# A pair of indirect transfers that waits for one landing of the pair in front

## What is computed

```python
x = L0_attn_x
x = x + 0.5 * _L0_ffn_ref(_layernorm(x, axis=-1), ...)
x = x + _L0_attn_ref(_layernorm(x, axis=-1), ...)
x = x + 0.5 * _L0_ffn_ref(_layernorm(x, axis=-1), ...)

def _L0_ffn_ref(x, gate_w, gate_b, w1, b1, w2, b2):
    logits = jnp.einsum('bsd,ed->bse', x, gate_w) + gate_b
    probs = jax.nn.softmax(logits, axis=-1)
    topk_vals, topk_idx = jax.lax.top_k(probs, K)
    h = jax.nn.relu(jnp.einsum('bsd,edh->bseh', x, w1) + b1)
    expert_out = jnp.einsum('bseh,eho->bseo', h, w2) + b2
    sel = jnp.take_along_axis(expert_out, topk_idx[..., None], axis=2)
    return jnp.sum(sel * topk_vals[..., None], axis=2)
```

## Time and profile before

| | |
|---|---|
| median of 3 runs | 1311.96 us (1311.27 to 1317.21) |
| the profiled execution | 1328.29 us |
| its span on the core | 1326.6 us |
| mean granted TensorE clock in it | 0.941 |
| busy: PE, ACT, DVE, POOL | 1202.2, 960.0, 688.8, 470.4 us |
| indirect transfers (software queue q0) | 31.49 MB, 7.9% of 16 engines |
| plain transfers (hardware queue q1) | 168.90 MB, 41.3% of 16 engines |

### The profile page before, as it was taken

One profiled execution on the slowest core, in us unless ns is written; L12 is line 12 of the kernel. 1 busy time (PEld: TensorE's weight loads), 2 busy tenths in 40 slices (PEclk: granted clock), 3 DMA queues, 4 the chain that ended last, 5 costly groups with the idle time before them and its releaser, 6 DMA issues.

```text
span 1326.6 us, 25770 instructions
## 1 busy us (share of the span) xinstructions
PE 1202.2 (91%) x8269; PEld 793.0 (60%) x8269; DVE 688.8 (52%) x2239; ACT 960.0 (72%) x2383; POOL 470.4 (35%) x528
## 2 busy tenths in 40 slices
PE   7988889989899998999999979998999989999696
PEld 2675576576466555666656546655755446666475
DVE  4357437456576543546573446544647636455133
ACT  3337759669699886887988857887868888797431
POOL 2012324344344434413443444343343442243333
PEclk9987998989989998999999979999998979999888
DMA  7305473664644264555557455626641145656561
GB/s 257 142 13 164 144 219 94 195 191 130 191 131 141 82 208 128 151 162 180 165 159 213 126 153 175 191 86 205 180 131 36 43 135 163 187 166 198 187 213 55
DMA packets 159849, 202.04 MB, mean 152 GB/s; under 512 B 16922, under 2 KB 103394, under 8 KB 159715
## 3 DMA queue, kind: packets, MB, share of 16 engines
q1 hardware_dynamic: 144196, 168.90, 41.3%
q0 software_dynamic: 15360, 31.49, 7.9%
q10 hardware_dynamic: 160, 0.01, 0.0%
HBM read 152.49 MB, written 47.84 MB: 151 GB/s over the span
## 4 chain that ended last, share of the span: by engine, by line
DMA 36%; PE 23%; issue 15%; POOL 14%; ACT 7%; DVE 4%; SPq 0%; POOLq 0%; DVEq 0%; ACTq 0%
PE psum L1548 21%; DMA Y<-results_A,posA 11%; DMA slots_C<-xnC,posC 9%; DMA Y<-results_C,posC 8%; POOL Y L1096 8%; DMA slots_A<-xnA,posA 7%; POOL slots_C L1076 3%; POOL slots_A L1076 3%; ACT psum L1177 3%; ACT probs L1168 2%; DVE neg_m L1502 1%; DVE X L1467 1%; ACT xnA L1133 1%; PE psum L1657 1%; PE psum L1625 0%
## 5 line engine op out<-in xcount | busy, mean ns | idle before, releaser
L1502 DVE TENSOR_REDUCE neg_m<-psum 128x1 f32<-128x512 f32 x512 | 317.0, 681 | 199.4 <-PE psum L1548 165.6
L1548 PE MATMUL psum<-nat 32*128 32x512 f32 x2048 | 393.8, 671 | 18.3 <-ACT psum L1177 13.6
L1177 ACT ACTIVATE psum<-psum,neg_m 128x512 f32<-128x512 f32 x512 | 341.5, 683 | 42.4 <-DVE neg_m L1502 35.7
L1168 ACT ACTIVATE probs<-psum 128x512 f32<-128x512 f32 x512 | 266.7, 632 | 35.1 <-PE psum L1548 33.2
L1548 PEld LDWEIGHTS psum<-nat 32*128 32x128 f32 x2048 | 144.7, 193 | 116.6 <-ACT psum L1177 36.1
L1076 POOL DMA_INDIRECT slots_A<-xnA,posA x120 | 117.5, 979 | 261.8 <-DMA slots_A<-xnA,posA 117.9
L1548 PEld LDWEIGHTS psum<-xg_T,wt 128*128 128x128 f32 x1296 | 161.3, 198 | 55.4 <-issue 15.7
L1548 PE MATMUL psum<-xg_T,wt 128*128 128x128 f32 x1296 | 179.1, 287 | 16.4 <-DMA wt<-packed 11.0
L1096 POOL DMA_INDIRECT Y<-results_C,posC x120 | 114.5, 954 | 207.5 <-DMA Y<-results_C,posC 138.5
L1096 POOL DMA_INDIRECT Y<-results_A,posA x120 | 114.7, 956 | 200.3 <-DMA Y<-results_A,posA 156.0
L1548 PEld LDWEIGHTS psum<-wt,hg 128*128 128x128 f32 x1296 | 158.8, 199 | 40.1 <-issue 14.3
(11 more groups left out here) (188 smaller groups left out, 1339.8 us busy)
## 6 DMA issues: line engine op xcount, KB each, us to landing
wt<-packed SPq DMA_DIRECT2D x324, 320.0 KB
xs<-slots_A SPq DMA_DIRECT2D x36, 256.0 KB
results_A<-ys SPq DMA_DIRECT2D x36, 256.0 KB
xs<-slots_C SPq DMA_DIRECT2D x36, 256.0 KB
results_C<-ys SPq DMA_DIRECT2D x36, 256.0 KB
X<-in_L_attn_x_dram SPq DMA_DIRECT2D x16, 256.0 KB, 7.0
out_dram<-X SPq DMA_DIRECT2D x16, 256.0 KB
packed<-probs SPq DMA_DIRECT2D x1, 2560.0 KB, 7.8
```

The source lines that it names most:

```text
L1168: act.activation(probs[:, kt, j, :], at.banks()[j][:], ACT.Exp).then_inc(a_done, 1)
L1177: act.activation(at.banks()[j][:], at.banks()[j][:], ACT.Exp, bias=neg_m[:, g, n, j:j + 1], accum_out=sums[:, g, n, j:j + 1]).then_inc(S[" ...
L1502: V_.tensor_reduce(neg_m[:, g, n, j:j + 1], at.banks()[j][:], AX.X, ALU.max, negate=True).then_inc(S["r_done"], 1)
L1548: return nc.tensor.matmul(dst, w, m, start=start, stop=stop)
```

## The change

Each place of each ring gets two semaphores in place of one, for the first (h = 0) and the second (h = 1) transfer of its pairs, and each of them counts 16 for a transfer. `apart` waits for the first transfer of the pair in front only. Whoever needs all the data (`xload` on SP, the overwriting of `xn` on ACT, `comb` on DVE) waits on both semaphores of the place, one after the other. `before` is now made from POOL's indirect steps alone; in this program POOL has no other planned steps, so it gives the same pairs. Which steps stand in which order on each engine, what each transfer moves, and all buffers are the same.

```diff
-        gy_in = [sem(f"gy_in{i}") for i in range(Y_RING)]
-        scat_in = {s: [sem(f"scat_in{s}{i}") for i in range(XN_RING)] for s in "AC"}
+        gy_in = [[sem(f"gy_in{i}_{h}") for h in range(2)] for i in range(Y_RING)]
+        scat_in = {s: [[sem(f"scat_in{s}{i}_{h}") for h in range(2)] for i in range(XN_RING)] for s in "AC"}
...
         def scattered(s, b):
-            return 32 * TILES * len([old for old in range(b % XN_RING, b + 1, XN_RING) if CHUNK_OF[s][old] != DENSE[s]])
+            return 16 * TILES * len([old for old in range(b % XN_RING, b + 1, XN_RING) if CHUNK_OF[s][old] != DENSE[s]])
...
                     for b in range(FIRST[c], FIRST[c] + CHUNKS[c]):
-                        sp.wait_ge(scat_in[s][b % XN_RING], scattered(s, b))
+                        for h in range(2):
+                            sp.wait_ge(scat_in[s][b % XN_RING][h], scattered(s, b))
...
-            before = {step: old for old, step in zip(order["POOL"], order["POOL"][1:])}
+            indirect = [step for step in order["POOL"] if step[2] in ("scat", "gat")]
+            before = {step: old for old, step in zip(indirect, indirect[1:])}
...
                 if old and old[2] == "scat":
                     s, c, t = old[0], old[1], old[3]
                     b = FIRST[c] + t // TILES
-                    pool.wait_ge(scat_in[s][b % XN_RING], scattered(s, b) - 32 * (TILES - 1 - t % TILES))
+                    pool.wait_ge(scat_in[s][b % XN_RING][0], scattered(s, b) - 16 * (TILES - 1 - t % TILES))
                 if old and old[2] == "gat":
                     i = comb_turn[old[:2]]
-                    pool.wait_ge(gy_in[i % Y_RING], ring_count(i, Y_RING, 32 * TILES) - 32 * (TILES - 1 - old[3]))
+                    pool.wait_ge(gy_in[i % Y_RING][0], ring_count(i, Y_RING, 16 * TILES) - 16 * (TILES - 1 - old[3]))
...
-                        scat_in[s][b % XN_RING], 16)
+                        scat_in[s][b % XN_RING][k], 16)
...
-                        gy_in[i % Y_RING], 16)
+                        gy_in[i % Y_RING][k], 16)
...
-                        act.wait_ge(scat_in[s][old % XN_RING], scattered(s, old))
+                        for h in range(2):
+                            act.wait_ge(scat_in[s][old % XN_RING][h], scattered(s, old))
...
-                dve.wait_ge(gy_in[i % Y_RING], ring_count(i, Y_RING, 32 * TILES))
+                for h in range(2):
+                    dve.wait_ge(gy_in[i % Y_RING][h], ring_count(i, Y_RING, 16 * TILES))
```

## The result

The changed kernel took 1432.87 us (median of 4 runs, 1416.87 to 1457.96) against 1314.59 us (1311.27 to 1322.22) for the kernel before in runs beside it: a ratio of 1.085, 95% interval 1.079 to 1.092. It is 8.5% slower where 1278 us and a gain were forecast. Later the same two kernels were measured again on two chips: 1.084 (1.078 to 1.089) on one, and **0.950** (0.943 to 0.957) on the other. Both answers are real, and the rest of this document is about why there are two.

The account below looks back on a forecast made before the run. It took POOL's serial pairs of indirect transfers, with PE nearly full, to bound the kernel. 18 + 9 + 10.7 - 1 = 37 us off the profiled execution, 34 off the median: 1312 - 34 = 1278 us, range 1252 to 1310.

Parts of the forecast that it names:

- The pair, 3.77 to 2.50 us: POOL's indirect transfer pairs: next pair no longer waits for the second landing, saving 1.27 us idle, 1.25 us taken.
- One more wait at 0.02 us for the consumers: DVE, SP and ACT: an added, already met wait costs 0.02 us each; 1 us put on the path.
- The middle, 18 + 9 us: Up to 1245 us: 18 us from closing PE's gaps, plus 9 us from a higher clock.
- the seven gaps of the earlier trace: PE's idle gaps before 1245 us, put down to late transfers: 24.5 us together, three quarters taken as gain.
- The clock: PE's lower granted clock after the gaps cost 18.6 us in six stretches; half, 9 us, taken as gain.
- The end, 10.7 us: After 1245 us: earlier scatters bring dense load and weights forward 8.0 us; last `comb` loses its 2.71 us wait.
- the wait for weights: At the end: PE's 7.52 us wait until 1263.25, behind the dense load, to end sooner with earlier scatters.
- The sum: Whole kernel: 18 + 9 + 10.7 - 1 = 37 us off the profiled execution, 34 off the median, 1278 us.
- more than I take: Rival: all 24.5 us of gaps, all 18.6 us of clock, 13 at the end; about 58 us, 1254; 6%.
- The slower rival: PE's weight waits: three indirect transfers delay weight loads, 55 us lost against 37 gained, 1330 us; 8%.
- The round robin: DMA engines alternate between queue rows packet by packet, so weight loads would lose turns to gathers; 1330 us by it.
- what the change adds: Forecast's cost part: one more wait per consumer, 30 on DVE, 30 on SP, under 30 on ACT; 1 us.

Follow-up runs that it names:

- e5: Changed kernel, but `apart` waits once, for the second transfer of the pair in front instead of the first; 1324.76 us, 1.003 of the kernel before.
- e1: Changed kernel, but `apart` waits for both transfers of the pair in front, on their two semaphores; 1409.79 us, 1.067 of the kernel before.
- e13: Changed kernel itself, unaltered, on a chip where SP's register instructions between weight loads never pass 38 ns (second sort); 1256.12 us, 0.950 of the kernel before.
- e16: Changed kernel, but behind scatters `apart` waits for the first and second transfer in turn, on a first-sort chip; 1296.96 us, 0.985 of the kernel before.
- e17: Changed kernel plus a POOL memset of 1024 unused columns before each pair, on a first-sort chip; 1262.56 us, 0.960 of the kernel before.
- e19: Changed kernel plus a POOL memset of 16 unused columns before each pair, on a first-sort chip; 1409.24 us, 1.073 of the kernel before.
- e18: Changed kernel itself, unaltered, on a chip where SP's register instructions reach hundreds of ns (first sort); 1425.23 us, 1.084 of the kernel before.
- e10: Changed kernel plus a POOL memset of 16 unused columns before each pair, on a second-sort chip; 1255.53 us, 0.954 of the kernel before.
- e11: Changed kernel, but no wait behind gathers (except first steps) and the second transfer awaited behind scatters, second-sort chip; 1256.13 us, 0.954 of the kernel before.
- e3: Changed kernel, but behind scatters `apart` waits for both transfers, on a first-sort chip; 1315.04 us, 0.992 of the kernel before.
- e6: Changed kernel, but behind scatters `apart` waits once, for the second transfer, on a second-sort chip; 1262.23 us, 0.954 of the kernel before.
- e12: Changed kernel, but behind every fourth scatter step `apart` waits for the second transfer, on a second-sort chip; 1254.04 us, 0.953 of the kernel before.
- e2: Changed kernel, but behind gathers `apart` waits for both transfers, on a first-sort chip; 1409.72 us, 1.060 of the kernel before.

## Why the prediction was wrong, and where it was right

**The pair, 3.77 to 2.50 us: right.** The shortest scatter pair is 2.54 us after, on both sorts, and the shortest gather pair, for which the forecast took the same figures, fell from 3.95 to 2.68 us. Under load, too: the mean interval of scatter pairs (those under 9 us) fell from 4.52 to 3.27 us, and that of gather pairs from 5.16 to 3.77, so 1.25 and 1.39 us against the 1.25 taken. The Trainium skill's fixed part ("DMA: Bandwidth & Descriptors", Anatomy of one DMA) would give the full 1.27 also under load, and these means agree with it.

**One more wait at 0.02 us for the consumers: right**, by e5 (1.003). The same price would have been wrong on POOL ahead of an indirect transfer, where e1 measured 0.43 us.

**The middle, 18 + 9 us: too small where it applies.** In e13, PE's last product with V ends at 1183.1 us instead of 1242.3, 59 us earlier, against the 27 forecast. None of the seven gaps of the earlier trace rows is left. Over the whole span PE's idle time fell from 124.4 to 82.8 us, by 41.6 where 28.7 (18 and 10.7) was forecast, so many gaps shorter than those I listed went too. The clock is the mis-sized term: the mean rose from 0.941 to 0.965, and PE's busy time fell by 29.5 us, where 9 were taken. I had halved a sum over the six stretches with the listed gaps, but even the whole of it, 18.6 us, is 11 us too little: the lower level (1.2 GHz of 2.4) that came with the pairs' lateness also stood outside these stretches.

**The end, 10.7 us: right in sum, wrong in one part.** From the end of the last product with V to the end of the span it took 84.3 us before, 72.4 in e13 and 74.7 after. SP's load of the dense experts' weights, issued 8.6 us after that product before, goes 1.5 us after it in e13, and the wait for `xs` of 4.53 us is gone. But the wait for weights, which was to go with it, stayed (PE and SP's queue in e13):

```profile
1197.36 1.23 PE L1552 MATMUL psum<-xg_T,wt 128*128 128x128 f32 x4 [7.20 <-DMA wt<-packed]
```
```profile
1184.59 0.39 SPq L950 DMA_DIRECT2D probs<-packed  x1
```

It was 7.52 us before: the weights came earlier and PE did, too. The last `comb` has no wait, as forecast (DVE in the profile after):

```profile
1422.57 2.30 DVE L1471 SCALAR_TENSOR_TENSOR X<-Y,gateC,X 128x128 f32<-128x128 f32 x8
```

**The sum.** On the second sort 64 us are gained where 34 were taken, and 1256 us lies by my "more than I take" (1254). The direction and the mechanism held there.

**The slower rival: right sign, wrong cause.** It had weights that come late behind a third transfer, and would decide beyond 24 us of waits for them. Before it was 23.9 us; in the profile after:

```profile
PE psum L1552 <- DMA wt<-packed: 11.0, 6, 7.8
```
```profile
PEld psum L1552 <- DMA wt<-packed: 11.4, 5, 8.1
```

These are 22.4 us in all. So the sign of this rival came out by luck. The weights are not later, and the indirect transfers' packets take hardly more of the transfer engines' time: 7.5% of 1427.6 us, or 107 us, against 7.9% of 1326.6, or 105. The round robin that the same page of the Trainium skill describes (Queues, rings and completion order) did no harm that these waits show.

**The step that failed** is in the part on what the change adds: it priced the added waits, and took it, without a row for it, that POOL's work itself costs the other engines nothing, at whatever density it is issued. No row of the kernel before could price that, since the kernel has no dense run; the rule I had set myself, to bound what the trace does not show from both sides, was applied to the landing and not to this. On a chip of the first sort it is the largest term. In the profile after 49 us of PE's idle time lie inside the five dense runs, and more behind them, as in the gap until 1143.47. Against e13 the idle time is 101 us longer and PE's busy time 71 us, the latter at a clock of 0.909 against 0.965: both add up to the 172 us between 1427.6 and 1255.5.

**What is shown and what is open.** Shown: the loss belongs to dense issue of indirect transfers on some chips (e16 against e17 on one chip, e19 and e18 on another, the two tables), while the same issue is free on others (e13, e10, e11). How large it is for the changed kernel against e17 rests on two chips of the first sort being alike. Shown, too, that it is not the DMA engines being full (14 to 17% in the windows), not the weights (22.4 us of waits) and not the consumers' waits (e5 on the second sort; e17 has them on the first and gains). The number under way is not it either, as far as rows go: in a dense run transfers begin 1.27 us apart and land after 2.2 us (median in e13's window), so two are under way, as in each pair of before. What slows down is each engine's own progress through its program, in steps of 0.70 us on SP and ACT: four SP issues in 15.14 us in place of 4.21. Single register instructions of hundreds of ns are no sign of it by themselves, since the kernel before has them too (707 ns). One candidate is the supply of instructions. The Trainium skill ("Runtime: NRT & Kernel Launch", Instruction fetch mechanics) says that each sequencer fetches its program in blocks over a DMA queue of its own, mostly hidden. This trace has 68 such loads of 16 KB in both kernels, with a median of 0.96 us after and 1.09 before, so the loads themselves are not slow. Between 1103 and 1151 us, through most of the stop, none takes place, and SP is slow at each single step; if a block came late, one step should be long and those behind it not. So this candidate fits badly. Whether the recording of the trace itself takes part, no run here shows. Which part of the chip is shared, and why chips differ, stays open. Not tried: e1 to e3 on the second sort, e5, e6, e11 and e12 on the first, the changed kernel and e17's on the same chip of the first sort, and dense gathers without dense scatters there. In e3 gathers that are fast but not dense cost little; what dense ones would cost is not known.

## What to carry to other kernels

A wait that looks like pure slack may be what keeps an engine's issues apart; before it goes, look whether the trace has any stretch with the density that would follow, and if it has none, that cost is unknown, in both signs. Where pairs of indirect transfers set the path, wait for the first landing and keep about 1 us of other work on POOL between pairs (3.4 us a pair): nearly all of the gain (0.954 and 0.960), on both chips where it was tried, one of each sort. And a result of some per cent that rests on one chip should be repeated on another, with the kernel before beside it.

## What the runs showed of the hardware that I had not expected

- Chips of the same type differ for the same program: 0.950 and 1.085 for the changed kernel, while the kernel before takes the same within 0.7% on all of them.
- Indirect transfers issued 1.27 us apart without a pause can stop the other engines on some chips: 17.5 us in which DVE and ACT execute nothing (e2), 15.2 us in the profile after. At 3.38 us a pair they do not (e17, 0.960).
- In such a stop an engine is not held once but slowed at each step: two kinds of SP's small instructions have a median of 700 and 710 ns there, against 18 and 29 ns for the same program on a chip of the second sort (e13).
- A second semaphore wait ahead of an indirect transfer costs POOL 0.43 to 0.48 us for each pair (e1, on one chip of the first sort), while on DVE, ACT and SP such waits cost nothing measurable (e5).
- The granted clock gave back three times what I took from the listed gaps: 29.5 us of PE's busy time for 41.6 us less of idleness.
